# Squares summed on TensorE, VectorE's steps alternated and weight loads in quarters, in the preparation of a two-layer kernel

## The chip, the cores and the metric

The kernel runs on one core of one Trainium2 chip. The metric is the device time of one launch in microseconds (us); a change of less than about 1% can't be told from no change here. All data is 32-bit float in memory; some operands are handed to TensorE in its single-pass form of the same width.

## The reference

The program is a two-layer network on 16 sequences of 512 tokens with 128 features (16 heads of 8). This case touches only what is prepared ahead of layer 0. Cut to what matters:

```python
xn = layernorm(x)                               # per token, 128 features
static = xn @ W.T                               # per token
k = rmsnorm(xn.reshape(B, L, 16, 8)) * k_norm_w # per token and head: root mean square of 8 values
for t in tokens:                                # per sequence and head, an 8 x 8 state S
    S = lam * S
    S = S + beta * outer(k[t], -static[t] - k[t] @ S)
    o[t] = k[t] @ S
x = x + layernorm(static + o) + ffn(xn)         # ffn: five weight matrices, three of them 512 wide
x = x + attention_layer_1(layernorm(x)) + ffn_1(...)
```

## The kernel before, in words

The program has two stages. `prepare` (line 125) makes, for each of the 16 sequences, five arrays of 128 rows by 512 tokens in HBM: the transposed normalized input (xnT), and P, K, R and fac, with which the recurrence over tokens can later be taken in blocks of four. It also turns the five weight matrices of the first feed-forward net into the form that TensorE wants. `recur_and_second_layer` then does the recurrence, both feed-forward nets and the second layer. Only `prepare` is changed.

**A sequence in `prepare`.** It is worked on in four engine-wide steps spread over four rounds. Every engine has one list of instructions, written as a loop over rounds `k`; in round k an engine works on the sequences k, k-1, k-2 and k-3, each at another stage, and semaphores with running counts tie the lists together. An engine never takes an instruction out of turn.

- Sequence k: VectorE takes mean and variance (`statistics` L590, `aggregate` L597), ScalarE the root (`root` L464), VectorE its reciprocal and the offset (L602, L603, L607), ScalarE applies both to the four tiles of 128 tokens (`norm` L470), giving p_xn.
- Still of p_xn: ScalarE squares it (`square` L477, tile p_sq), VectorE sums the squares of each head's 8 values (`square_sums` L613, tile p_ssq of 64 columns), ScalarE takes the root (`root_mean` L481, p_rms), VectorE the reciprocal and the product with p_xn (L618, L623, p_keys).
- TensorE transposes p_xn (`normed` L743, PSUM bank p_ps_x), ScalarE copies it out (L486, p_xnT) and SyncE stores it. TensorE transposes the keys with the places of each block of four sorted (`keys` L751), ScalarE copies them (L494, p_kT). TensorE multiplies xnT by W (`static` L758), ScalarE copies that into p_rr (L499).
- Within a block of four tokens the answer needs products of keys one, two and three places apart (d = 1, 2, 3). VectorE makes them (`products` L634, tile p_prod, three instructions of 384, 256 and 128 columns, one semaphore count behind the last), TensorE sums them over a head with a block matrix of ones (`couplings` L766, bank p_ps_n), ScalarE copies them to p_coup (L509). VectorE solves the triangle for R and GpSimd for P: three sweeps j = 0, 1, 2, each a product (L265) and a sum (L269), 384, 256 and 128 columns wide, and each waits for the one before it. GpSimd also makes P's start (`scaled` L382) and K (`outgoing` L390).
- ScalarE squares the keys (L503), TensorE sums and spreads them (`factors` L776, bank p_ps_f), ScalarE turns them into fac (L516).

**The weights.** Eleven groups of four 128 x 128 squares, one per round from k = 2 on: TensorE transposes a group into the same bank p_ps_f (`weights` L786), ScalarE rounds it (`upper` L521), VectorE makes the rest (`lower` L651). Since fac and the weights share p_ps_f, `weights` of round k waits until ScalarE has read fac of round k out of it (`reuse(pe, fac_ok, ...)`), and all of TensorE's list waits with it. The two 512 x 512 matrices arrive as one load of 1 MB each, issued at k = 1 and k = 4.

**TensorE's round** is: static, couplings, keys, normed, factors, weights. **ScalarE's round** is: std, kT, xnT, rr, rms, fac, xn, w_hi, sq, k2, coup.

**The queue of stores.** SyncE issues nearly all transfers, in the order of its list: in round k the stores of P(k-4), xnT(k-1), fac(k-3), K(k-2), then the load of x(k+2), the store of R(k-3), and weights and small constants. P, K and R each have a small transfer besides (`first_p`, `first_k`, `first_r`: the first 64 columns). A wait in this list holds all that stands behind it. Each array has two buffers, so ScalarE may write p_rr of sequence n only when the store of R(n-2) has landed, and likewise for the others.

`count(each, more)` turns a sequence's number into the count that a semaphore has reached; `at(s, stage)` calls a stage if that sequence exists.

## Time and profile before

| | |
|---|---|
| median of 3 runs | 816.92 us (811.57 to 817.61) |
| the profiled execution | 813.44 us |
| its span, first to last instruction | 811.7 us |
| granted TensorE clock over the span | 0.974 |
| `prepare` | about the first 150 us |
| TensorE / VectorE / ScalarE / GpSimd busy, whole span | 90% / 90% / 73% / 79% |

A timeline gives each instruction's start and duration; neighbours in time that are alike are merged, with their count behind an x. A wait stands in brackets with what ended it. "p_" in front of a tile means that it belongs to `prepare`.
### The profile page before, as it was taken

The numbers are of one execution on the slowest core, as the hardware profiler recorded it, in microseconds if no ns is written. First come the engines' busy times: TensorE is split into PE (matmuls) and PEld (weight loads), VectorE is DVE, ScalarE is ACT, GpSimd is POOL, SyncE is SP. The second block draws the span as 40 slices with busy tenths as digits, with TensorE's granted clock in tenths as the row PEclk, the third lists the DMA queues.
The fourth block names the chain that finished last, engine by engine and source line by source line (L and its number), as shares of the span: only waits on it lengthen the run. The fifth ranks groups of instructions, "written<-read, shape, count | busy, mean of one in ns | idle before, by whom it ended". The sixth has DMA issues, their size and how long they took to land.

```text
span 811.7 us, 13074 instructions
## 1 busy us (share of the span) xinstructions
PE 731.4 (90%) x3325; PEld 515.9 (64%) x3325; DVE 727.2 (90%) x2036; ACT 591.0 (73%) x1363; POOL 644.1 (79%) x640
## 2 busy tenths in 40 slices
PE   4979788699999999999999999986699999999998
PEld 2434344467787888778887788762356666666565
DVE  5979898899999999998998979996578888899887
ACT  7878776789778887887888788785565566666631
POOL 3767788697977897879888779766789778889873
PEclk9999999799999999999999999997999999999999
DMA  6678665600512416161151160510623202211001
GB/s 163 200 240 259 202 207 195 162 14 16 142 39 54 89 39 142 39 143 39 39 103 40 39 143 26 160 32 13 182 69 118 66 27 66 66 53 39 2 27 40
DMA packets 136073, 75.75 MB, mean 93 GB/s; under 512 B 74826, under 2 KB 118860, under 8 KB 136012
## 3 DMA queue, kind: packets, MB, share of 16 engines
q1 hardware_dynamic: 134956, 74.58, 32.9%
q10 hardware_dynamic: 1056, 0.52, 0.2%
q8 instruction: 18, 0.29, 0.1%
q14 instruction: 43, 0.35, 0.1%
HBM read 39.86 MB, written 33.55 MB: 90 GB/s over the span
## 4 chain that ended last, share of the span: by engine, by line
PE 61%; ACT 10%; POOL 4%; issue 3%; DVE 2%; POOLq 0%; DVEq 0%; ACTq 0%
PE f_ps L2266 15%; PE f_ps L2268 10%; PE f_ps L2402 7%; PE f_ps L2303 6%; PE f_ps L2403 6%; PE f_ps L2379 4%; PE f_ps L2273 4%; ACT L1896 2%; ACT f_a L1896 1%; PE r_rec L2431 1%; ACT f_hh L1911 1%; PE r_rec L2437 1%; ACT f_h L1910 1%; DVE l_qs L1321 1%; PE r_rec L2421 1%
## 5 line engine op out<-in xcount | busy, mean ns | idle before, releaser
L1646 POOL TENSOR_TENSOR l_kv<-l_qkv 128x1024 f32<-128x1024 f32 x64 | 124.9, 1956 | 21.6 <-PE f_ps L2403 19.6
L1247 DVE TENSOR_REDUCE r_rec<-r_pg 128x32 f32<-128x288 f32 x256 | 113.0, 441 | 0.6 <-ACT r_pg L1865 0.6
L1518 POOL TENSOR_TENSOR f_hl<-f_h,f_hh 128x512 fp32r<-128x512 f32 x64 | 82.1, 1311 | 33.1 <-ACT f_hh L1911 33.1
L1321 DVE TENSOR_TENSOR l_qs<-f_ps,l_qd 128x1024 f32<-128x1024 f32 x64 | 78.1, 1221 | 27.4 <-PE f_ps L2403 20.8
L1259 DVE TENSOR_REDUCE r_gain<-r_kw 128x64 f32<-128x256 f32 x256 | 102.3, 400 | 0.0
L2266 PE MATMUL f_ps<-f_hh,w_hi 128*128 128x512 f32 x256 | 101.2, 395 | 0.4 <-ACT f_b L1900 0.4
L2266 PE MATMUL f_ps<-f_gh,w_hi 128*128 128x512 f32 x256 | 100.0, 390 | 1.3 <-POOL f_gl L1518 1.2
L1526 POOL TENSOR_TENSOR f_g<-f_a,f_b 128x512 f32<-128x512 f32 x64 | 82.2, 1296 | 22.1 <-ACT f_b L1900 22.1
L1267 DVE SCALAR_TENSOR_TENSOR r_rec<-r_rec,lam,r_gain 128x64 f32<-128x64 f32 x256 | 70.1, 274 | 19.2 <-ACT r_w L1876 19.2
L1518 POOL TENSOR_TENSOR f_gl<-f_g,f_gh 128x512 fp32r<-128x512 f32 x64 | 82.2, 1297 | 4.8 <-ACT f_gh L1906 4.6
L1328 DVE TENSOR_REDUCE l_o_in<-l_qs 128x128 f32<-128x1024 f32 x64 | 77.2, 1211 | 0.6
L2402 PE MATMUL f_ps<-l_kv,tri 128*128 128x512 f32 x128 | 67.8, 611 | 8.3 <-POOL l_kv L1646 5.0
L2268 PE MATMUL f_ps<-f_hl,w_hi 128*128 128x512 f32 x192 | 75.0, 391 | 0.0
L2268 PE MATMUL f_ps<-f_gl,w_hi 128*128 128x512 f32 x192 | 74.7, 389 | 0.0
L2049 ACT ACTIVATE l_qkv<-f_ps 128x384 f32<-128x384 f32 x64 | 31.3, 489 | 56.0 <-PE f_ps L2379 55.3
L1906 ACT ACTIVATE f_gh<-f_g 128x512 fp32r<-128x512 f32 x64 | 41.7, 652 | 38.9 <-POOL f_g L1526 38.1
L2266 PE MATMUL f_ps<-f_xh,w_hi 128*128 128x512 f32 x128 | 53.7, 419 | 14.9 <-ACT f_a L1896 14.9
L2403 PE MATMUL f_ps<-l_kv,tri 128*128 128x512 f32 x128 | 66.9, 605 | 0.0
L1910 ACT ACTIVATE f_h<-f_ps,t 128x512 f32<-128x512 f32 x64 | 44.6, 697 | 22.9 <-PE f_ps L2273 22.6
L2303 PEld LDWEIGHTS f_ps<-w,f_e 128*128 128x128 f32 x512 | 59.7, 192 | 0.8
L2303 PE MATMUL f_ps<-w,f_e 128*128 128x128 f32 x512 | 59.7, 275 | 0.0
L2379 PE MATMUL f_ps<-l_w_second,l_xnT 128*128 128x384 f32 x128 | 54.4, 508 | 3.4 <-ACT l_qkv L2049 2.1
(227 smaller groups left out, 2103.7 us busy)
## 6 DMA issues: line engine op xcount, KB each, us to landing
scratch_xnT<-p_xnT SPq DMA_DIRECT2D x16, 256.0 KB, 2.2
scratch_K<-p_kout SPq DMA_DIRECT2D x16, 256.0 KB, 2.4
scratch_fac<-p_fac SPq DMA_DIRECT2D x16, 256.0 KB, 2.0
scratch_R<-p_rr SPq DMA_DIRECT2D x16, 256.0 KB, 2.9
scratch_P<-p_pp SPq DMA_DIRECT2D x16, 256.0 KB, 2.3
first_x<-scratch_xnT SPq DMA_DIRECT2D x16, 256.0 KB, 3.5
first_xt<-in_L_attn_x_dram SPq DMA_DIRECT2D x16, 256.0 KB, 3.0
scratch_W<-r_w SPq DMA_DIRECT2D x16, 256.0 KB, 4.0
```

The lines of the kernel that those rows point to most:

```text
L1247: dve.tensor_reduce(w_here(g, blk), pg[q][:, at, :, :, :].rearrange("p (v g) i k -> p v g i k", g=G)[:, :, g, :, :], AX.X, ALU.add).then_i ...
L1259: dve.tensor_reduce(of_group(g, gain), of_group(g, kw), AX.X, ALU.add).then_inc(gain_ok, 1)
L1321: dve.tensor_tensor(qs[s % 2][:, :].rearrange("p (h v k) -> p h v k", h=H, k=DH), score_banks(s)[:, :, :].rearrange("p a (h v k) -> p (a h ...
L1518: pool.tensor_tensor(lower, full, upper.bitcast(F32), ALU.subtract).then_inc(done, 1)
L1526: pool.tensor_tensor(g_f[:, j, :], a_f[:, j, :], b_f[:, j, :], ALU.mult).then_inc(gate_ok, 1)
L1646: pool.tensor_tensor(dst, k, v, ALU.mult).then_inc(kv_ok, 1)
L2266: nc.tensor.matmul(bank, c.w_hi[:, weights[k], :], upper[k], start=k == 0, stop=False)
L2268: nc.tensor.matmul(bank, c.w_hi[:, weights[k], :], lower[k], start=False, stop=False)
L2303: ins = nc.tensor.matmul(y_at[:, tokens], e_f[:, k, tokens], c.w3[:, k, :], start=False, stop=t == NT - 1 and k == NB - 1)
L2379: nc.tensor.matmul(ps_q[:, 0:3, :].rearrange("p a b -> p (a b)"), xnT[m % XTS][:, t, :], w_second[:, 0:3 * P], start=True, stop=True).then ...
L2402: nc.tensor.matmul(to[:, 0, :], c.tri[:, :], kv[s % 2][:, 0, :], start=True, stop=True)
L2403: nc.tensor.matmul(to[:, 1, :], c.tri[:, :], kv[s % 2][:, 1, :], start=True, stop=True).then_inc(tri_mm, 1)
```

## The change

1. The squares of a head are summed on TensorE. ScalarE squares the transposed tile straight out of the bank p_ps_x, TensorE multiplies it with 16 columns of the block matrix of ones (four matmuls with 16 moving columns, the squares being the stationary side) back into p_ps_x, and ScalarE takes the root from there. VectorE's sum is gone. In TensorE's round the sums stand between `factors` and `weights`; the next transposes into p_ps_x wait for the root.
2. Half the norm: ScalarE normalizes two tiles of a sequence, VectorE the other two, with a semaphore of its own.
3. VectorE's steps alternate: products, sweeps, scale and norm are interleaved, `statistics` and `aggregate` of sequence k+1 are taken at the end of round k, around the keys.
4. The products and couplings are counted place by place, d = 3 first: TensorE may start on one when it is made, and ScalarE copy it.
5. The weights arrive in quarters of 256 KB (512-byte rows), one per round, each issued when the second before it has landed.
6. SyncE's round is K(k-2), xnT(k-1), P(k-3), fac(k-3), R(k-3), load x(k+2), weights. P(k-3) was stored a round later.

```diff
@@ SyncE @@
                     if s.off >= 2:
                         sp.wait_ge(xn_ok, s.count(1, -1))
+                        sp.wait_ge(xn_half, s.count(1, -1))
...
+                def load_weights(g):
+                    if 2 + 2 <= g < NG - 1:
+                        sp.wait_ge(*arrived(g - 2))
+                    sp.dma_start(*mats[g]).then_inc(arrived(g)[0], 16)
...
                 for k in range(B + 1):
-                    at(of(k - 4), store_p)
+                    at(of(k - 2), store_keys)
                     at(of(k - 1), store_normed)
+                    at(of(k - 3), store_p)
                     at(of(k - 3), store_factors)
-                    at(of(k - 2), store_keys)
+                    at(of(k - 3), store_r)
                     at(of(k + 2), load)
-                    at(of(k - 3), store_r)
                     if k in MATS_AT:
-                        sp.dma_start(*mats[MATS_AT[k]]).then_inc(mat_in[MATS_AT[k]], 16)
+                        load_weights(MATS_AT[k])
@@ ScalarE @@
-                    for t in range(NT):
+                    for t in range(NT // 2):
...
-                def square(l):
-                    act.wait_ge(ssq_ok, l.count(1, 1))
-                    act.wait_ge(xn_ok, l.count(1, 1))
-                    act.activation(sq[:, :, :], xn[l.slot][:, :, :], ACT.Square).then_inc(sq_ok, 1)
+                def square(m):
+                    act.wait_ge(ssq_ok, m.count(1, 1))
+                    act.activation(sq[:, :, :], ps_x[:, :, :], ACT.Square).then_inc(sq_ok, 1)
...
                 def root_mean(m):
                     act.wait_ge(ssq_ok, m.count(1, 2))
-                    act.activation(rms[:, :], ssq[:, :], ACT.Sqrt, bias=c.eps_rms[:, :], scale=1.0 / DH).then_inc(rms_ok, 1)
+                    act.activation(rms[:, :], ps_x[:, 0, 0:NT * H], ACT.Sqrt, bias=c.eps_rms[:, :], scale=1.0 / DH).then_inc(rms_ok, 1)
@@ VectorE @@
+                def norm(l):
+                    dve.wait_ge(nm_ok, l.count(1, 1))
+                    dve.wait_ge(x_tr, l.count(1, 1))
+                    for t in range(NT // 2, NT):
+                        ins = dve.tensor_scalar(xn[l.slot][:, t, :], x_in[l.slot][:, t, :], rstd[:, t:t + 1], nm[:, t:t + 1],
+                                                ALU.mult, ALU.add)
+                    ins.then_inc(xn_half, 1)
...
-                    at(of(k - 1), square_sums)
-                    at(of(k - 3), solve, 0)
+                    at(of(k - 3), solve_product, 0)
                     at(of(k), scale)
+                    at(of(k - 3), solve_sum, 0)
                     at(of(k), offset)
-                    at(of(k - 3), solve, 1)
-                    at(of(k - 2), products)
-                    at(of(k - 3), solve, 2)
+                    at(of(k - 3), solve_product, 1)
+                    at(of(k - 2), products, 0)
+                    at(of(k - 3), solve_sum, 1)
+                    at(of(k), norm)
+                    at(of(k - 2), products, 1)
+                    at(of(k - 3), solve_product, 2)
+                    at(of(k - 2), products, 2)
+                    at(of(k - 3), solve_sum, 2)
                     at(of(k - 1), inverse_rms)
+                    at(of(k + 1), statistics)
                     at(of(k - 1), keys)
+                    at(of(k + 1), aggregate)
@@ TensorE @@
                 def normed(m):
                     pe.wait_ge(xn_ok, m.count(1, 1))
+                    pe.wait_ge(xn_half, m.count(1, 1))
                     pe.wait_ge(xT_ok, m.count(1, 1))
+                    pe.wait_ge(rms_ok, m.count(1, 1))
...
+                def square_sums(m):
+                    pe.wait_ge(sq_ok, m.count(1, 1))
+                    for t in range(NT):
+                        ins = nc.tensor.matmul(ps_x[:, 0, t * H:(t + 1) * H], sq[:, t, :], c.head_ones[:, 0:P:DH], start=True, stop=True)
+                    ins.then_inc(ssq_ok, 1)
...
                 def couplings(n):
-                    pe.wait_ge(prod_ok, n.count(1, 3))
                     pe.wait_ge(coup_ok, n.count(1, 1))
-                    pe.wait_ge(r_step, n.count(SWEEPS, 2 * SWEEPS))
...
+                    for i, d in enumerate(PLACED):
+                        pe.wait_ge(prod_ok, n.count(BLK - 1, 2 * (BLK - 1) + i + 1))
+                        pe.wait_ge(r_step, n.count(SWEEPS, SWEEPS + 2 * i + 1))
...
                     at(of(k - 1), normed)
                     at(of(k - 3), factors)
+                    at(of(k - 1), square_sums)
```

TensorE, one round from the copy of a weight group to the next, before (p_ps_f is the shared bank, p_k the squared keys, p_nath a group of the 512-wide weights):

```order
L786 MATMUL p_ps_f<-ident,p_nath 128x128 x4
L758 MATMUL p_ps_s<-p_xnT,ws_t 128x512
L766 MATMUL p_ps_n<-p_prod,head_ones 128x384
L766 MATMUL p_ps_n<-p_prod,head_ones 128x8x32
L766 MATMUL p_ps_n<-p_prod,head_ones 128x8x16
L751 MATMUL p_ps_k<-by_place,p_keys 128x128 x4
L743 MATMUL p_ps_x<-ident,p_xn 128x128 x4
L776 MATMUL p_ps_f<-p_k,head_ones 128x512
```

and with the change (line numbers are those of the changed file):

```order
L823 MATMUL p_ps_f<-ident,p_nath 128x128 x4
L796 MATMUL p_ps_s<-p_xnT,ws_t 128x512
L804 MATMUL p_ps_n<-p_prod,head_ones 128x8x16
L804 MATMUL p_ps_n<-p_prod,head_ones 128x8x32
L804 MATMUL p_ps_n<-p_prod,head_ones 128x384
L783 MATMUL p_ps_k<-by_place,p_keys 128x128 x4
L775 MATMUL p_ps_x<-ident,p_xn 128x128 x4
L813 MATMUL p_ps_f<-p_k,head_ones 128x512
L789 MATMUL p_ps_x<-head_ones,p_sq 128x16 x4
```

The four sums (p_ps_x<-head_ones,p_sq) stand between factors and weights, and the couplings come smallest first.

ScalarE, from the first root of a round to the rounding of the weights, before:

```order
L464 ACTIVATE p_std<-p_mv,eps_ln 128x4
L494 ACTIVATE p_kT<-p_ps_k,knw 128x512
L486 ACTIVATE p_xnT<-p_ps_x 128x512
L499 ACTIVATE p_rr<-p_ps_s 128x512
L481 ACTIVATE p_rms<-p_ssq,eps_rms 128x64
L516 ACTIVATE p_fac<-p_ps_f,gate 128x512
L470 ACTIVATE p_xn<-p_x,p_nm,p_rstd 128x128 x4
L521 ACTIVATE w_hi<-p_ps_f 128x512
```

and with the change:

```order
L483 ACTIVATE p_std<-p_mv,eps_ln 128x4
L512 ACTIVATE p_kT<-p_ps_k,knw 128x512
L504 ACTIVATE p_xnT<-p_ps_x 128x512
L495 ACTIVATE p_sq<-p_ps_x 128x512
L517 ACTIVATE p_rr<-p_ps_s 128x512
L499 ACTIVATE p_rms<-p_ps_x,eps_rms 128x64
L534 ACTIVATE p_fac<-p_ps_f,gate 128x512
L489 ACTIVATE p_xn<-p_x,p_nm,p_rstd 128x128 x2
```

The squares moved from behind w_hi to behind xnT, and their root now stands behind a sum that TensorE makes after factors; the norm has two instructions and not four, and the rounding of the weights (w_hi) follows it as before.

SyncE's queue, a round in which weights are loaded, before:

```order
L322 DMA first_p<-p_pp 16x8x64
L293 DMA scratch_P<-p_pp 128x512
L293 DMA scratch_xnT<-p_xnT 128x512
L293 DMA scratch_fac<-p_fac 128x512
L311 DMA first_k<-p_kout 16x8x64
L293 DMA scratch_K<-p_kout 128x512
L289 DMA p_x<-in_L_attn_x_dram 128x4x128
L316 DMA first_r<-p_rr 16x8x64
L293 DMA scratch_R<-p_rr 128x512
L344 DMA p_nath<-in_L_ffn_h_w_dram 128x4x512
```

and with the change:

```order
L330 DMA first_k<-p_kout 16x8x64
L307 DMA scratch_K<-p_kout 128x512
L307 DMA scratch_xnT<-p_xnT 128x512
L341 DMA first_p<-p_pp 16x8x64
L307 DMA scratch_P<-p_pp 128x512
L307 DMA scratch_fac<-p_fac 128x512
L335 DMA first_r<-p_rr 16x8x64
L307 DMA scratch_R<-p_rr 128x512
L303 DMA p_x<-in_L_attn_x_dram 128x4x128
L312 DMA p_nath<-in_L_ffn_h_w_dram 128x4x128
```

P of the round stands ahead of fac, R and the load of x; it was the first entry of the next round.

## Rows read from the trace of the kernel before

**Rows 1.** Busy time by stretch: us, engines' busy time (instructions), granted clock, DMA.
```profile
65.00:72.70 7.70, 6.78 (x28) 3.43 (x27) 7.31 (x25) 6.66 (x17) 6.37 (x8) 1.00 0.82 250
119.00:121.00 2.00, 2.00 (x4) 0.84 (x3) 1.86 (x7) 1.91 (x5) 1.92 (x4) 0.50 0.61 222
```

**Rows 2.** Timeline of ScalarE, the copies of the transposed tile; start, duration.
```profile
47.05 0.60 ACT L486 ACTIVATE p_xnT<-p_ps_x 128x512 f32<-128x512 f32 x1
...
58.29 0.60 ACT L486 ACTIVATE p_xnT<-p_ps_x 128x512 f32<-128x512 f32 x1
...
81.35 0.61 ACT L486 ACTIVATE p_xnT<-p_ps_x 128x512 f32<-128x512 f32 x1
...
92.31 0.60 ACT L486 ACTIVATE p_xnT<-p_ps_x 128x512 f32<-128x512 f32 x1
```

**Rows 3.** Timeline of TensorE, one group from 68.26 to 75.95 us.
```profile
68.26 0.63 PE L786 MATMUL p_ps_f<-ident,p_nath 128*128 128x128 f32 x4 [0.92 <-ACT p_fac L516]
68.72 1.96 PE L758 MATMUL p_ps_s<-p_xnT,ws_t 128*128 128x512 f32 x2
70.51 1.48 PE L766 MATMUL p_ps_n<-p_prod,head_ones 128*128 128x384 f32 x6
...
73.15 1.88 PE L776 MATMUL p_ps_f<-p_k,head_ones 128*128 128x512 f32 x2
75.95 0.30 PE L786 MATMUL p_ps_f<-ident,p_nath 128*128 128x128 f32 x1 [0.92 <-ACT p_fac L516]
```

**Rows 4.** Timeline of ScalarE beside it, 72 to 76 us.
```profile
72.08 0.93 ACT L509 ACTIVATE p_coup<-p_ps_n 128x384 f32<-128x384 f32 x3 [0.91 <-PE p_ps_n L766]
...
74.30 0.60 ACT L499 ACTIVATE p_rr<-p_ps_s 128x512 f32<-128x512 f32 x1
74.79 0.34 ACT L481 ACTIVATE p_rms<-p_ssq,eps_rms 128x64 f32<-128x64 f32 x1
75.12 0.69 ACT L516 ACTIVATE p_fac<-p_ps_f,gate 128x512 f32<-128x512 f32 x1
```

**Rows 5.** Group of VectorE's sums, 0 to 180 us: count, busy us, mean ns.
```profile
L613 DVE TENSOR_REDUCE p_ssq<-p_sq 128x64 f32<-128x512 f32 x16 | 10.8, 672 | 1.1 <-ACT p_sq L477 1.1
```

**Rows 6.** The same view of the whole span, a stream of load and matmul pairs.
```profile
L2303 PEld LDWEIGHTS f_ps<-w,f_e 128*128 128x128 f32 x512 | 59.7, 192 | 0.8
L2303 PE MATMUL f_ps<-w,f_e 128*128 128x128 f32 x512 | 59.7, 275 | 0.0
```

**Rows 7.** Timeline of ScalarE: the two long waits for a store.
```profile
50.28 0.60 ACT L499 ACTIVATE p_rr<-p_ps_s 128x512 f32<-128x512 f32 x1 [2.62 <-DMA scratch_R<-p_rr]
...
84.20 0.60 ACT L499 ACTIVATE p_rr<-p_ps_s 128x512 f32<-128x512 f32 x1 [2.25 <-DMA scratch_R<-p_rr]
```

**Rows 8.** Timeline of TensorE: a pause, and the matmuls behind it.
```profile
117.80 2.12 PE L758 MATMUL p_ps_s<-p_xnT,ws_t 128*128 128x512 f32 x2 [2.00 <-issue]
119.74 2.19 PE L766 MATMUL p_ps_n<-p_prod,head_ones 128*128 128x384 f32 x6
```

**Rows 9.** Timeline of GpSimd: first, fourth last and last step of one solution.
```profile
65.41 1.00 POOL L265 TENSOR_TENSOR p_tmp_p<-p_coup,p_pp 128x384 f32<-128x384 f32 x1 [1.17 <-ACT p_coup L509]
...
70.53 1.04 POOL L382 TENSOR_TENSOR p_pp<-p_kT,pfac 128x512 f32<-128x512 f32 x1 [0.51 <-DMA scratch_P<-p_pp]
...
72.06 0.46 POOL L269 TENSOR_TENSOR p_pp<-p_pp,p_tmp_p 128x128 f32<-128x128 f32 x1
```

**Rows 10.** Timeline of SyncE's queue: issue of the stores of R.
```profile
70.28 0.58 SPq L316 DMA_DIRECT2D first_r<-p_rr  x1
70.90 0.59 SPq L293 DMA_DIRECT2D scratch_R<-p_rr  x1
```

**Rows 11.** DMA issues: KB each, median us from issue to landing.
```profile
scratch_R<-p_rr SPq DMA_DIRECT2D x16, 256.0 KB, 2.9
...
p_nath<-in_L_ffn_h_w_dram SPq DMA_DIRECT2D x2, 1024.0 KB, 7.1
```

**Rows 12.** Waits over the span: us in total, times, longest us.
```profile
PE p_ps_f L786 <- ACT p_fac L516: 13.7, 10, 3.4
```

More of the change, by code:

```diff
@@ L139, in prepare @@
     POWERS_AT = 13
+    PLACED = range(BLK - 1, 0, -1)
     with ctx:
@@ L260, in earlier, with sweep_product @@
             return slice(0, (BLK - d) * BSEG)
-        def sweep(eng, n, ap, couplings, tmp, step, j):
+        def sweep_product(eng, n, ap, couplings, tmp, step, j):
             rest = BLK - 1 - j
@@ L506, in couplings @@
                     act.wait_ge(p_step, n.count(SWEEPS, SWEEPS))
[L507 to L508 removed]
+                    for i, d in enumerate(PLACED):
+                        act.wait_ge(n_mm, n.count(BLK - 1, BLK + i))
                         ins = act.activation(coup[n.slot][:, d - 1, :, earlier(d)], in_ps[:, d - 1, :, earlier(d)], ACT.Copy)
```

95 lines of the change are left out of this document (49 added, 46 removed).

## The prediction, blind

> **What bounds the kernel now.** I read the profile's page first: only the first 150 us or so are `prepare`, and the change touches nothing behind them, so the question is how long one round of `prepare` takes and how often it is disturbed. Then I followed one instruction that every sequence has once, ScalarE's copy of the transposed tile: from 58.29 to 81.35 us three rounds pass, so an undisturbed round is 23.06 / 3 = 7.69 us; two rounds took 11.24 (47.05 to 58.29) and 10.96 us (81.35 to 92.31) [rows 2].
>
> Next the busy time of every engine in one round of 7.70 us: VectorE 7.31, TensorE 6.78, ScalarE 6.66, GpSimd 6.37 [rows 1]. By that VectorE looks like the bound, and a reader would expect that taking its sum away (0.67 us a round [rows 5]) pays. But the share isn't the argument; the wait is. TensorE's timeline shows its round without a hole from the transposes of the weights at 68.26 to the end of factors at 73.15 + 1.88 = 75.03, which is 6.77 us, and then one wait of 0.92 us for ScalarE's fac, after which the next round starts at 75.95 [rows 3]. 6.77 + 0.92 = 7.69: this loop is the round. Within the wait, fac starts at 75.12, takes 0.69, and TensorE starts 0.14 behind it [rows 3, 4]. VectorE is nearly as full, but TensorE is never seen waiting for it in this stretch. The same wait stands ten times in the trace, 13.7 us in all [rows 12]: once for each weight group but the first.
>
> The two long rounds each begin with a wait of ScalarE's static copy (p_rr) for an older store of R, 2.62 and 2.25 us [rows 7]. The first lies behind a load of 1 MB, and those took 7.1 us to land against 2.9 for a store of R [rows 11]. They cost 11.24 - 7.69 = 3.55 and 10.96 - 7.69 = 3.27 us, more than the wait, and a later pause shows why: after 2.00 us without work TensorE's couplings took 2.19 us where they took 1.48 undisturbed, at a granted clock of 0.50, which is 1.2 and not 2.4 GHz [rows 1, 3, 8].
>
> **The change part by part.** Everything is put on the profiled execution, 813.4 us (span 811.7 and 1.7 around it), and then on the median of the runs, 816.9, which lies 3.5 above it.
>
> *Squares on TensorE.* Four matmuls are four pairs of 32-bit records with a load each, so 8 loads of 128 x 128 and 8 matmuls of 16 moving columns. The trace has no matmul that narrow with a full load. Nearest is the stream of 512 loads and 512 matmuls of 128 columns: both engines' parts are busy for the same 59.7 us, 0.117 us a pair [rows 6]. Bounds: nothing, if they were free; and if load and matmul followed one another, 8 x (0.192 + 0.275) = 3.7 us [rows 6]. I take the stream's price, since here the loads are the same and the matmuls shorter, and one pair less, since the first load can go in under factors: 7 x 0.117 = 0.82 us. Where it lies decides. The order puts the sums between factors and weights, in TensorE's wait for fac, which would hide them if ScalarE could make fac meanwhile. It can't: in ScalarE's list the root stands ahead of fac, and the root now waits for the sums. So after the sums come the root (fac started 0.33 us behind it, 74.79 to 75.12 [rows 4]) and then fac, and only then the weights. The wait of 0.92 stays whole, and the round becomes 7.69 + 0.82 + 0.33 = 8.84 us. That holds for the ten groups of [rows 12]: 10 x 1.15 = 11.5 us. The first sequence has the same step ahead of its first keys, when nothing else runs: 1.15 us more, bounds 0 and 2.4 (twice it, since TensorE starts at 1.2 GHz and the list of VectorE now has the third tile's statistics ahead of the keys). In the last rounds there are no weights and TensorE has pauses of its own (the 2.00 us of [rows 8]); I take nothing, at most 4 x 0.82 = 3.3.
>
> The Trainium skill speaks against even this price: TensorE: Matmul & The Clock Gate, in the part on packing small matmuls ("What overlaps and what doesn't"), has it that a weight load overlaps a running matmul only when it goes to another row group. By that rule the eight pairs would follow one another, and the sum would be the upper bound above and not 0.82. The stream of [rows 6] uses all rows in each load and still overlaps, so the trace doesn't agree, and I keep the rule as a rival with a small chance.
>
> *VectorE's sum gone, half the norm on it, steps alternated, couplings place by place.* VectorE loses 0.67 [rows 5] and gains two normalizations of 128 columns, at most half of that instruction over 512 columns, 0.34, and at least nothing. ScalarE loses two of four normalizations and copies the couplings as they come. All this shortens ScalarE's and VectorE's lists, and neither is what TensorE's loop waits on except through root and fac, so I count it at nothing. What hides it is the loop above: at 8.84 us a round VectorE's 7.31 leaves 1.5 us. If the loop were not there, up to 0.4 us a round would be to be had.
>
> *Quarters.* The same bytes, in eight loads of 256 KB where there were two of 1 MB. The store of R no longer queues behind 7.1 us of one load, so the first long round should be an ordinary one: -3.4 us. The second has no 1 MB load near it and I leave it in. Bounds: 0 and -6.8.
>
> *P ahead of R in SyncE's queue.* R(k-3) now waits for P(k-3). GpSimd needs from the couplings to P: 65.41 to 72.52, 7.1 us, of which 0.51 was a wait for P's own earlier store [rows 9], so 6.6. Then SyncE issues first_p, P, fac, first_r and R, 0.62 us apart [rows 10], and R lands after 2.9 [rows 11]: 4 x 0.62 + 2.9 = 5.4 at most, about 5.2 as fac's issue is short. ScalarE may then copy p_rr of the sequence two later; from that copy to the end of its couplings were 73.01 + 7.69 - 74.30 = 6.4 us [rows 2, 4], now some 0.5 less as they are copied while they are made. Together 17.7 us for two rounds, 8.85 a round: level with the 8.84 above. So the move costs nothing yet, but has used up the slack: every microsecond that R lands later costs half of one in each round. It gains GpSimd its 0.5 us, which nobody waits for. Value 0, bounds 0 and +11.5 (a landing 2.3 us late in ten rounds, as the waits of [rows 7] show is possible).
>
> Sum: 11.5 + 1.15 - 3.4 = +9.2 us: 822.6 by the profiled execution, 826.1 by the median.
>
> **The rivals.**
>
> *The sums are cheap and both stalls go.* With 16 columns a pair costs half the stream's price, so the round is 7.69 + 0.41 + 0.33 = 8.43, and the longer round gives all stores time: 11 x 0.74 - 6.8 = +1.3, 818. For it: the transfers get 10% more time a round. Against it: the second stall had no large load to blame. Chance 0.20.
>
> *The clock falls in every round.* TensorE's stretch from the end of factors would be 0.82 us of very narrow matmuls and 1.25 us of waiting, 2.1 in all, much like the 2.00 us after which the clock was 0.50 [rows 1, 8]. Couplings would take 0.7 and static 0.16 more [rows 3, 8]: 10 x 0.86 = 8.6, so 834.7. Against it: the narrow matmuls are work of a kind. Chance 0.15.
>
> *R lands late.* The queue's slack is gone, and a landing 2.3 us late costs 1.15 a round: 826.1 + 11.5 = 837.6. For it: the waits of [rows 7]. Against it: rounds are longer and loads smaller. Chance 0.12.
>
> *VectorE was the bound (the other side).* If TensorE's wait for fac only mirrors VectorE, which was busy 7.31 of 7.70, then the sum's 0.67 less the new 0.34 is gained in each of 15 rounds, -5.0, with both stalls -6.8: 805.1. Its place is TensorE's 0.92 us wait, its condition that the sums and the root fit into it, and it decides once a round is below 7.6. Against it is the order of ScalarE's list. Chance 0.08.
>
> *Load and matmul don't overlap.* 3.7 us for the sums, so 11 x (3.7 + 0.33) - 3.4 = +41, 858. Chance 0.03; the page's rule named above would give this.
>
> **How the numbers follow.** The forecast case has 0.42 and its own range, 820 to 832, from the bounds of start and second stall. A change below 1% (8 us, 808.8 to 825.1) can't be told from none. Slower by more: the part of the forecast case above 825.1, 0.25, the clock 0.15, the late store 0.12, the series 0.03: 0.55. Within 1%: 0.17 of the forecast case and the cheap sums' 0.20: 0.37. Faster: 0.08. The range that leaves out no more than 2 in 10 runs from 812 to 840: it leaves out the faster case, the series, and the ends where two costs add up.
>
> **What would show it.** Right: an undisturbed round of about 8.8 us between two copies of the transposed tile; TensorE's wait ahead of the weights still there, 1.2 us, behind about 0.8 us of sums; ScalarE's root waiting for the sums ten times; VectorE idle a microsecond and more a round, waiting for the couplings; no long round at the former 1 MB load. Wrong: a round of 7.7 or less, a root that doesn't wait, a wait for R's store in most rounds (the late store), or a granted clock of 0.50 behind the sums.

## The result, and the profile after

The changed kernel takes 840.24 us (median of 4 runs, 838.93 to 841.48); the kernel before took 814.75 beside it (4 runs). The ratio is 1.032, 95% interval 1.030 to 1.035: slower, where 826.1 with a range of 812 to 840 had been forecast. Its profiled span is 837.2 us.

First the page's row of a round, found as before by ScalarE's copy of the transposed tile (timeline of ScalarE after the change, as [rows 2] before):

```profile
66.41 0.59 ACT L504 ACTIVATE p_xnT<-p_ps_x 128x512 f32<-128x512 f32 x1
...
76.56 0.59 ACT L504 ACTIVATE p_xnT<-p_ps_x 128x512 f32<-128x512 f32 x1
...
86.76 0.59 ACT L504 ACTIVATE p_xnT<-p_ps_x 128x512 f32<-128x512 f32 x1
```

A round takes 10.15 to 10.24 us, not 8.84. The last of the 16 copies starts at 151.85 us; before it was 130.35. So 21.5 of the 25.5 us of span have come by then. The long rounds of [rows 2] are gone: the rounds from the second to the twelfth creep from 9.38 up to 10.24 and none stands out; the last three take 7.55, 9.55 and 7.07.

TensorE's timeline of one round after the change, as [rows 3]:

```profile
69.67 0.63 PE L823 MATMUL p_ps_f<-ident,p_nath 128*128 128x128 f32 x4 [1.07 <-DMA p_nath<-in_L_ffn_h_w_dram]
70.14 1.96 PE L796 MATMUL p_ps_s<-p_xnT,ws_t 128*128 128x512 f32 x2
71.92 2.74 PE L804 MATMUL p_ps_n<-p_prod,head_ones 128*128 128x128 f32 x6
74.45 1.33 PE L783 MATMUL p_ps_k<-by_place,p_keys 128*128 128x128 f32 x8
75.62 0.60 PE L775 MATMUL p_ps_x<-ident,p_xn 128*128 128x128 f32 x4
76.06 1.87 PE L813 MATMUL p_ps_f<-p_k,head_ones 128*128 128x512 f32 x2
77.75 1.01 PE L789 MATMUL p_ps_x<-head_ones,p_sq 128*128 128x16 f32 x8
79.83 0.63 PE L823 MATMUL p_ps_f<-ident,p_nath 128*128 128x128 f32 x4 [1.07 <-ACT p_fac L534]
```

Read by the distance between starts. The sums are where the order put them and take 1.0 us; behind them TensorE waits 1.07 us, for fac as a rule (the first bracket names the quarter of weights, which landed last that time). That part is as forecast. What is not: couplings hold TensorE for 74.45 - 71.92 = 2.53 us, where they took 1.31 undisturbed, and keys for 1.17, where they took 0.89. The windows of the same execution say why (columns: window, length, busy time and count of TensorE, its loads, VectorE, ScalarE, GpSimd, then the granted clock, DMA share, GB/s):

```profile
78.80:79.80 1.00, 0.00 (x0) 0.00 (x0) 1.00 (x4) 1.00 (x3) 0.92 (x3) 1.00 0.16 38
81.00:82.00 1.00, 1.00 (x2) 0.21 (x1) 1.00 (x5) 0.61 (x2) 0.71 (x2) 0.92 0.43 164
82.00:83.00 1.00, 1.00 (x5) 0.83 (x4) 1.00 (x6) 0.22 (x1) 0.00 (x0) 0.50 0.00 0
83.00:84.00 1.00, 1.00 (x4) 0.61 (x3) 0.06 (x1) 0.44 (x2) 0.00 (x0) 0.50 0.64 217
84.00:85.00 1.00, 1.00 (x4) 0.70 (x3) 0.00 (x0) 0.14 (x1) 0.00 (x0) 0.50 0.96 351
```

The clock is still 1.00 in the pause, falls two microseconds behind it, under static, and is 0.50, 1.2 GHz, while couplings run. Couplings hold TensorE for 2.53 us in every round with weights from 50 us on; in the two rounds before that for 1.74 and 2.31 (at 33 and 42 us). With that and with keys, which go from 0.89 to 1.24, the rounds creep up. From 40 to 120 us the clock's mean is 0.83; before it was 0.94:

```profile
40.00:120.00 80.00, 72.12 (x272) 42.98 (x272) 62.34 (x200) 49.38 (x112) 49.87 (x65) 0.83 0.64 204
```

The waits after the change (us in total, times, longest):

```profile
POOL p_tmp_p L267 <- ACT p_coup L527: 46.3, 15, 3.7
...
DVE p_ps_t L267 <- ACT p_coup L527: 26.9, 13, 2.4
...
ACT p_rms L499 <- PE p_ps_x L789: 10.6, 13, 2.0
PE p_ps_f L823 <- ACT p_fac L534: 9.7, 9, 1.1
```

VectorE and GpSimd wait for couplings; the root waits for the sums thirteen times; the wait of [rows 12] is still there, 9.7 us in nine. By this profile the clock looked like the whole miss. A granted clock of 0.50 behind the sums is one of the prediction's own signs of being wrong. The runs show a second cause beside it.

### The profile page after: what moved, and what is told of

Its sections match the earlier page's. It is cut to its first block, busy times and chain, and to the rows that moved or that the text cites. A ratio compares the mean times of both kernels' runs of the same rounds, so it can differ in the third digit from the quotient of the medians.

```text
span 837.2 us, 13366 instructions
## 1 busy us (share of the span) xinstructions
PE 760.8 (91%) x3453; PEld 542.3 (65%) x3453; DVE 733.4 (88%) x2052; ACT 582.8 (70%) x1331; POOL 643.2 (77%) x640
## 4 chain that ended last, share of the span: by engine, by line
PE 59%; ACT 9%; POOL 6%; issue 3%; DVE 1%; POOLq 0%; DVEq 0%
PE f_ps L2304 14%; PE f_ps L2306 9%; PE f_ps L2440 6%; PE f_ps L2341 6%; PE f_ps L2441 6%; PE f_ps L2311 4%; PE f_ps L2417 4%; ACT L1934 2%; POOL l_kv L1684 2%; PE r_rec L2475 1%; PE r_rec L2469 1%; ACT f_hh L1949 1%; ACT f_a L1934 1%; ACT f_h L1948 1%; PE f_ps L2448 1%
## 5 line engine op out<-in xcount | busy, mean ns | idle before, releaser
L267 POOL TENSOR_TENSOR p_tmp_p<-p_coup,p_pp 128x384 f32<-128x384 f32 (+2 forms) x48 | 35.9, 748 | 46.6 <-ACT p_coup L527 46.3
```

## The experiments

Each run has its own runs of the kernel before beside it; ratios are against those, with 95% intervals. "Round" is the distance between two copies of the transposed tile. The diffs are cut to the lines that the argument needs, with some lines joined: declarations, semaphores and the like are left out.

### The clock: e1, e2, e4

**e1_wide**: the sums move 128 columns instead of 16.

```diff
-matmul(ps_x[:, 0, t * H:(t + 1) * H], sq[:, t, :], c.head_ones[:, 0:P:DH], ...)
+matmul(ps_x[:, t, :], sq[:, t, :], c.head_ones[:, :], ...)
...
-act.activation(rms[:, :], ps_x[:, 0, 0:NT * H], ACT.Sqrt, ...)
+act.activation(rms[:, :] ..., ps_x[:, :, 0:P:DH], ACT.Sqrt, ...)
```

The root now reads every 8th column of the sums (DH is 8; the expectation says every 16th).

> The sums of squares move 128 columns instead of 16 (the whole matrix of head ones; the root reads every 16th column). The loads are the same eight, TensorE does more in them. Theory 1 (the sums as such cost about 1 us a round, and the rest of the loss is TensorE's clock, which falls to 0.50 in static and couplings behind sums with hardly any columns and the pause after them): if the wider sums count as work, the granted clock stays 1.00 in couplings, couplings to keys go back from 2.53 to about 1.3 us, and a round takes about 8.9 instead of 10.2: some 822 us. Theory 2 (the pause of 1.1 us behind the sums lets the clock fall, whatever the sums are): round 10.2, 840 us. Theory 3 (the long couplings are a wait for VectorE or ScalarE and not the clock): 840 us, and the clock in them may be either.

Measured 828.5 us, ratio 1.016 (1.012 to 1.019). Most rounds are 8.76. TensorE's timeline in one of them:

```profile
76.09 0.63 PE L823 MATMUL p_ps_f<-ident,p_nath 128*128 128x128 f32 x4 [1.07 <-ACT p_fac L534]
76.56 1.96 PE L796 MATMUL p_ps_s<-p_xnT,ws_t 128*128 128x512 f32 x2
78.34 1.48 PE L804 MATMUL p_ps_n<-p_prod,head_ones 128*128 128x128 f32 x6
79.66 1.05 PE L783 MATMUL p_ps_k<-by_place,p_keys 128*128 128x128 f32 x8
...
82.68 1.09 PE L789 MATMUL p_ps_x<-head_ones,p_sq 128*128 128x128 f32 x8
84.85 0.63 PE L823 MATMUL p_ps_f<-ident,p_nath 128*128 128x128 f32 x4 [1.07 <-ACT p_fac L534]
```

The same eight loads, eight times the columns, the same pause of 1.07 us, and the sums cost 1.1 us instead of 1.0. But couplings are back at 79.66 - 78.34 = 1.32 us, and under them the granted clock is 1.00:

```profile
78.80:79.80 1.00, 1.00 (x6) 0.71 (x5) 0.66 (x3) 0.66 (x2) 0.00 (x0) 1.00 0.15 33
```

So more work for TensorE made the kernel 12 us faster. Theory 2 (the pause alone does it) and theory 3 (a wait) fall. The time is not theory 1's 822 either: behind the second round four took 9.15 to 11.0 us, and ScalarE waited ten times for R's store, 11.8 us in all. In one of these the pause is longer, and there the wide sums don't hold the clock either:

```profile
66.41 0.63 PE L823 MATMUL p_ps_f<-ident,p_nath 128*128 128x128 f32 x4 [1.80 <-DMA p_nath<-in_L_ffn_h_w_dram]
...
68.66 2.40 PE L804 MATMUL p_ps_n<-p_prod,head_ones 128*128 128x128 f32 x6
70.89 1.05 PE L783 MATMUL p_ps_k<-by_place,p_keys 128*128 128x128 f32 x8
```

Behind a pause of 1.80 us couplings hold TensorE for 2.23 us, and the granted clock of the two microseconds from 67 us is 0.54.

**e2_fac_first**: one swap in ScalarE's list.

```diff
-at(of(k - 1), root_mean)
 at(of(k - 3), factors)
+at(of(k - 1), root_mean)
```

> One swap in ScalarE's list: fac (factors of k-3) is copied before the root of k-1, so that TensorE's weights don't wait for a fac that stands behind the root. Theory 1 (the loss is the order root ahead of fac, the pause that it makes and the clock that falls behind that pause): sums run while fac is copied, the pause of 1.07 us is gone, the clock stays 1.00 in couplings, and a round takes 7.8 to 8.0 us: 811 to 816 us, at or below the kernel before. Theory 2 (the sums take TensorE's time and make the clock fall by themselves): the pause is gone but the clock still falls, round 9.2, about 829. Theory 3 (VectorE's half norm, or its list, sets the round): the root is 0.7 us later, keys with it, round 10 or more, 838 and more.

Measured 828.3, ratio 1.018 (1.014 to 1.022): theory 2's number, with theory 1's mechanism. Rounds alternate, 7.68, 9.46, 7.86, 11.14, 7.69, 9.96. In a short one TensorE has no pause and the clock stays 1.00, as theory 1 has it. Each long one begins with p_rr waiting for R's store (eight times, 11.0 us). No theory had named that.

**e4_sums_alone**: the kernel before with only part 1 of the change.

```diff
 # TensorE, round k
 at(of(k - 3), factors)
+at(of(k - 1), square_sums)
 # VectorE, round k
-at(of(k - 1), square_sums)
```

> The kernel before with the first part of the change alone: squares from the transposed tile in PSUM, summed by four matmuls on TensorE between factors and weights, root ahead of fac. Theory 1 (this part alone makes the loss): round of 10.0 to 10.3, granted clock 0.50 in couplings, 838 to 844 us, more where the loads of 1 MB are still in the way. Theory 2 (it takes the other parts as well): 8.8 a round, clock 1.00 in couplings, 825 to 830 us.

Measured 837.8, ratio 1.029 (1.026 to 1.032); rounds creep to 10.24, as in the changed kernel. Theory 1, 0.2 us below its range: this part alone gives nearly the whole loss. The two loads of 1 MB are still in this kernel and no round stands out, so it is the longer round and not the smaller loads that takes the stalls away.

### The queue: e3, e5 to e8, e11

**e3_sums_vector**: the change without its first part (squares from p_xn, summed on VectorE).

```diff
 # TensorE, round k
 at(of(k - 3), factors)
-at(of(k - 1), square_sums)
 # VectorE, round k
+at(of(k - 1), square_sums)
 at(of(k - 3), solve_product, 0)
```

> The change without its first part: the squares come from the normalized tile again and are summed on VectorE; half norm on VectorE, alternated steps, couplings place by place, quarters and SyncE's order stay. Theory 1 (the sums on TensorE with the root ahead of fac are the whole loss): round 7.7, no long round at the load, 812 to 816 us. Theory 2 (the half norm on VectorE costs, 1.78 us where 0.34 was the bound): VectorE has 7.31 + 1.5 us of work a round and sets it, round 8.5 to 8.9, 824 to 832 us.

Measured 828.5, ratio 1.017 (1.015 to 1.020). The number is theory 2's, the mechanism is not: rounds are not 8.5 but 7.63 and 9.99, 7.87 and 10.15, in turn. Its rows in a long one, ScalarE, TensorE, and SyncE's queue ahead of it:

```profile
70.90 0.59 ACT L506 ACTIVATE p_xnT<-p_ps_x 128x512 f32<-128x512 f32 x1
73.28 0.60 ACT L519 ACTIVATE p_rr<-p_ps_s 128x512 f32<-128x512 f32 x1 [1.79 <-DMA scratch_R<-p_rr]
```

```profile
74.84 1.08 PE L825 MATMUL p_ps_f<-ident,p_nath 128*128 128x128 f32 x4 [2.57 <-ACT p_fac L536]
75.71 1.99 PE L798 MATMUL p_ps_s<-p_xnT,ws_t 128*128 128x512 f32 x2
77.52 2.74 PE L806 MATMUL p_ps_n<-p_prod,head_ones 128*128 128x128 f32 x6
```

```profile
66.48 0.41 SPq L307 DMA_DIRECT2D scratch_xnT<-p_xnT  x1
68.52 0.60 SPq L341 DMA_DIRECT2D first_p<-p_pp  x1
69.16 0.58 SPq L307 DMA_DIRECT2D scratch_P<-p_pp  x1
69.79 0.43 SPq L307 DMA_DIRECT2D scratch_fac<-p_fac  x1
70.26 0.55 SPq L335 DMA_DIRECT2D first_r<-p_rr  x1
70.86 0.59 SPq L307 DMA_DIRECT2D scratch_R<-p_rr  x1
```

SyncE stands from 66.9 to 68.5 at first_p, for GpSimd; R is issued at 70.86, 0.04 ahead of the copy of the transposed tile. In the kernel before it was issued at 70.90 [rows 10] with that copy at 73.66, so 2.8 us ahead. R lands late, p_rr waits 1.79, fac is late, TensorE pauses 2.57, and behind that pause the clock falls and couplings take 2.53. This round takes 82.23 - 70.90 = 11.33 us, 3.5 more than the 7.87 ahead of it; the other long rounds with weights, behind waits of 1.2 to 1.9 us, take 10.0 to 10.2, 2.3 more.

**e11_queue_alone**: the kernel before with SyncE's order of the changed one and nothing else.

```diff
-at(of(k - 4), store_p); at(of(k - 1), store_normed); at(of(k - 3), store_factors)
-at(of(k - 2), store_keys); at(of(k + 2), load); at(of(k - 3), store_r)
+at(of(k - 2), store_keys); at(of(k - 1), store_normed); at(of(k - 3), store_p)
+at(of(k - 3), store_factors); at(of(k - 3), store_r); at(of(k + 2), load)
...
 # behind the last round
-store_p(of(B - 3)); store_factors(of(B - 2)); store_keys(of(B - 1)); store_r(of(B - 2)); store_p(of(B - 2))
+store_keys(of(B - 1)); store_p(of(B - 2)); store_factors(of(B - 2)); store_r(of(B - 2))
```

The second half of the diff, the stores behind the last round, belongs to the change too.

> The kernel before with SyncE's order of the changed kernel and nothing else. Theory 1 (R's store, behind P's wait for GpSimd, lands too late wherever rounds want to be 7.7): p_rr waits for it in every second round, TensorE's pause there grows over 2 us, the clock falls to 0.50 behind it, rounds alternate between 7.7 and 10: 826 to 832 us. Theory 2 (the queue has slack without the other parts): 812 to 818 us.

Measured 831.2, ratio 1.020 (1.017 to 1.023): theory 1. Rounds 7.68 and 10.5 to 11.7 in turn, seven waits for R's store of 18.5 us in all. An order of issues, with no work added or taken away, costs 17 us.

**e5_fac_first_old_queue** and **e6_vector_old_queue**: e2 and e3 with SyncE's order of the kernel before, that is with the diff of e11 read backwards.

> fac ahead of the root on ScalarE, and SyncE's order of the kernel before (P a round later, behind nothing; R behind the load). With fac first alone every second round was long (7.7 and 9.5 to 11.1 us), and each long one began with ScalarE's p_rr waiting for the store of R. Theory 1 (the store of R behind P's wait for GpSimd causes these): the waits for R's store all but go, rounds are 7.7 to 7.9 us, clock 1.00 in couplings, 806 to 812 us, below the kernel before. Theory 2 (the long rounds come from the half norm on VectorE or the alternated steps, which make R late itself): they stay, 826 to 830 us.

> Sums back on VectorE, and SyncE's order of the kernel before. Theory 1 (the store of R behind P's wait is what made every second round 10 us there): rounds of 7.7 to 7.9, 806 to 814 us. Theory 2 (VectorE is full with the half norm, which took 1.78 us: 7.31 + 1.5): rounds of 8.5 and more, 822 to 830 us.

e5: 813.9, ratio 1.001 (1.000 to 1.002), level with the kernel before rather than below it. Rounds are 7.70 and 7.87 with one of 10.03, and p_rr waits for R once, 0.8 us. e6: 817.8, ratio 1.005 (1.003 to 1.006); nine rounds are 7.6 to 8.0 and five stay long, 9.2 to 10.5, here and there and no longer in turn. The queue made the alternation in both: theory 1, with its numbers 2 to 4 us too low.

TensorE's weights in a short round of e3, where VectorE makes the sums, have the old wait of 0.92 us in front of them:

```profile
65.32 0.63 PE L825 MATMUL p_ps_f<-ident,p_nath 128*128 128x128 f32 x4 [0.92 <-ACT p_fac L536]
```

In a short round of e5 the sums fill it:

```profile
43.79 1.01 PE L790 MATMUL p_ps_x<-head_ones,p_sq 128*128 128x16 f32 x8
44.89 0.63 PE L824 MATMUL p_ps_f<-ident,p_nath 128*128 128x128 f32 x4
```

No bracket stands behind the weights: TensorE no longer waits. So the sums fit into the wait, as my rival on the other side had it, once fac does not stand behind the root. They gain nothing there, since they are as long as the wait was. The clock holds in these rounds, with the same 16 columns in the sums: couplings take 48.45 - 47.13 = 1.32 us in the round of these rows.

**e7_old_queue**: the changed kernel with only SyncE's order put back (the same lines as in e5).

> The changed kernel with SyncE's order of the kernel before and nothing else. Theory 1 (in the changed kernel R's store isn't late, since its rounds of 10.2 give it time; the pause behind the sums and the clock make the rounds): rounds of 10.2 as before, 838 to 841 us. Theory 2 (the late store of R is in every round): 828 us or less.

Measured 832.0, ratio 1.024 (1.022 to 1.025), between the two. The rounds up to the thirteenth are the same, 10.2 us, so a round of 10.2 does give R's store time and theory 1 holds for them. What it missed is the end: the fourteenth round takes 8.17 instead of 9.55, and from the last copy of the transposed tile to the last store of P go 168.23 - 150.18 = 18.1 us instead of 172.99 - 151.85 = 21.1. In the changed kernel SyncE stands first for K (issued at 164.05) and then for P (167.48) before it comes to the last stores, and p_rr waits for R's store, 1.23 and 2.13 us, where it waits 0.20 and 0.51 in e7. Behind such a wait TensorE pauses and the clock falls here too (the changed kernel, ScalarE and TensorE):

```profile
155.06 0.60 ACT L517 ACTIVATE p_rr<-p_ps_s 128x512 f32<-128x512 f32 x1 [2.13 <-DMA scratch_R<-p_rr]
155.75 2.02 PE L796 MATMUL p_ps_s<-p_xnT,ws_t 128*128 128x512 f32 x2 [1.71 <-issue]
157.59 2.74 PE L804 MATMUL p_ps_n<-p_prod,head_ones 128*128 128x128 f32 x6
```

The last store of P is issued 172.99 - 168.23 = 4.8 us earlier in e7, of 7.7 us of span; the other 2.9 lie behind `prepare`. From that store to the end of the span go 664.2 us in the changed kernel and 661.3 in e7. The kernel before has 663.1 and the other profiled executions lie between 661 and 664.5, so the 2.9 are not shown to come from the queue.

**e8_fac_first_r_first**: fac first, and of SyncE's new order only P moved behind R.

```diff
-at(of(k - 3), store_p)
 at(of(k - 3), store_factors)
 at(of(k - 3), store_r)
+at(of(k - 3), store_p)
```

> fac ahead of the root on ScalarE, and in SyncE's new order only P moved: behind fac and R instead of ahead of them. Theory 1 (P ahead of R is the harmful part of the new order): as with the whole old order, rounds of 7.7 to 7.9, 806 to 812 us. Theory 2 (K's stores, now first in the round, hold the queue for GpSimd just as well: SyncE waited 22.9 us for K and 19.7 us for P): between the two, 815 to 828 us.

Measured 815.2, ratio 1.002 (1.000 to 1.004). The number stands at the lower end of theory 2's range; but it is 1.3 us above e5 and 13.1 below e2, and the rounds are theory 1's, 7.68 to 7.98 from the third to the thirteenth with one of 10.06. So moving P behind R takes nearly all of the queue's cost away. K's stores at the head of the round hold SyncE for 35.2 us in thirteen waits, and p_rr still waits for R only twice, 1.9 us in all. What K's place costs by itself is not shown, since e8 also has R ahead of the load and e5 has not.

### Both causes taken away: e16

**e16_wide_old_queue**: the edit of e1 and SyncE's old order together.

> The changed kernel with the wide sums (128 columns) and SyncE's order of the kernel before: with the clock held and R's store early, this is the case that I had forecast. Theory 1: rounds of 8.77 throughout, none of 10 to 11, and the 6 to 8 us that the old order gave the end: 816 to 822 us. Theory 2 (the clock falls in some rounds for another reason than the wait for R's store): 824 to 828.

Measured 821.05, ratio 1.009 (1.007 to 1.012), span 819.3. Ten rounds of 8.76, none longer behind the second; the clock never leaves 1.00 between 40 and 120 us:

```profile
40.00:120.00 80.00, 71.40 (x311) 40.09 (x309) 71.77 (x231) 56.89 (x129) 57.79 (x75) 1.00 0.71 229
```

This is the case that I had forecast: 8.76 for 8.84 a round, and 6.6 us above the kernel before for +9.2.

### The other parts: e9, e10, e15

**e9_quarters_alone**: the kernel before, 1 MB loads cut into quarters.

```diff
-MATS_AT = {1: 2, 4: 3, 7: 4}
+MATS_AT = {g - 1: g for g in range(2, NG)}
...
-(nath[:, 0, :, :], io["L0_ffn_h1_w"].rearrange("(o p) i -> p o i", p=P)),
+mats += [(nath[:, w, :, i * P:(i + 1) * P], rows[:, :, i * P:(i + 1) * P]) for i in range(NB)]
```

> The kernel before with its two loads of 1 MB cut into eight of 256 KB, one a round, and nothing else. Theory 1 (my term of the prediction: the first long round has the 1 MB load ahead of R's store, the second has not): one long round instead of two, -3.4 us, 811 us by the runs here. Theory 2 (both long rounds come from R's store being at the edge whatever is loaded): no gain, 812 to 816 us.

Measured 814.7, ratio 0.9993 (0.9975 to 1.0012): theory 2. The long rounds 11.24 and 10.96 become 9.11 and 10.55, but the second round goes from 7.26 to 8.27.

**e10_half_norm_alone**: the kernel before, two of four tiles normalized on VectorE.

```diff
 # VectorE, round k
 at(of(k - 2), products)
+at(of(k), norm)
 at(of(k - 3), solve, 2)
 # ScalarE's norm
-for t in range(NT):
+for t in range(NT // 2):
```

> The kernel before with two of the four tiles normalized on VectorE (behind the products), and nothing else. Theory 1 (those two steps take 0.8 us each beside GpSimd's, so VectorE's 7.31 of 7.69 becomes 8.9 and it sets the round): rounds of 8.4 to 8.9, 820 to 830 us. Theory 2 (they take long only where VectorE is in no hurry): 0.34 each, rounds of 7.7 to 8.0, 813 to 818 us.

Measured 823.0, ratio 1.010 (1.007 to 1.012): theory 1, at the low end. Its group of VectorE's half norm (count, busy us, mean ns):

```profile
L623 DVE TENSOR_SCALAR p_xn<-p_x,p_rstd,p_nm 128x128 f32<-128x128 f32 x24 | 13.4, 596 | 0.0
```

1.19 us a round for the two; rounds are mostly 8.0 to 9.8, and from 20 to 125 us VectorE is busy for 99.2 of the 105. Where VectorE is full, this part costs 8.6 us. In the changed kernel VectorE idles 2 us a round, so the part should be hidden there; no run takes it out of the changed kernel. e6, which has the half norm with the alternated steps, the couplings place by place and the quarters, is 4.3 us above the kernel before, so these three together give back some 4 of the 8.6.

**e15_sums_alone_fac_first**: e4 with fac ahead of the root, by the swap of e2.

> The kernel before with the sums on TensorE and fac ahead of the root, so with neither the alternated steps nor the couplings place by place. It tells what these two do. Theory 1 (nothing, TensorE's own work of 7.7 us sets the round): as fac first with the old queue, rounds of 7.7 to 7.9 and now and then a long one by the loads of 1 MB, 814 to 819 us. Theory 2 (the later root needs the alternated steps, or the couplings wait for all products together and TensorE gets a new pause there): rounds of 8.3 and more, 822 us and more.

Measured 818.5, ratio 1.006 (1.004 to 1.009): theory 1. Undisturbed rounds are 7.70 here and 7.70 and 7.87 in e5, so the alternated steps and the couplings place by place gain nothing in the steady round. But e5 also has the half norm and the quarters, which e15 has not, so what each does by itself isn't shown. Over the whole kernel e5 is 4.6 us faster, by its first round (8.29 for 9.12) and because fewer rounds are long. Against e4, 837.8, the one swap is worth 19 us.

### Attempts to beat both: e12, e13, e14

**e12_normed_behind_factors**: kernel before, quarters, and TensorE's transposes of the normalized tile moved into its wait.

```diff
-at(of(k - 1), normed)
 at(of(k - 3), factors)
+at(of(k - 1), normed)
```

> An attempt to beat both: the kernel before with the quarters, and with the transposes of the normalized tile moved on TensorE from ahead of factors to behind them (fac ahead of the copy of the transposed tile on ScalarE), so that they lie in TensorE's wait of 0.92 us for fac. Theory 1 (the round is TensorE's 6.77 us of work and that wait): TensorE's round becomes 6.77 + 0.48 = 7.25, VectorE with 7.31 sets it, rounds of 7.3 to 7.45, 3 to 4 us less: 807 to 810. Theory 2 (the copy of the transposed tile, now behind fac, comes late for static and makes the wait there): rounds of 7.7 or more, 812 and more.

Measured 817.0, ratio 1.003 (1.002 to 1.005): theory 2's number and its place, static, but another copy than it names. The wait for fac halves, and static gets one of its own. Static also waits until p_rr has emptied its bank, and with fac and the transposed tile ahead of it that copy (65.09 + 0.60) ends 0.10 us before static starts, 0.5 behind that of the transposed tile:

```profile
64.86 0.63 PE L800 MATMUL p_ps_f<-ident,p_nath 128*128 128x128 f32 x4 [0.48 <-ACT p_fac L530]
65.79 2.02 PE L772 MATMUL p_ps_s<-p_xnT,ws_t 128*128 128x512 f32 x2 [0.30 <-issue]
```

```profile
64.61 0.60 ACT L500 ACTIVATE p_xnT<-p_ps_x 128x512 f32<-128x512 f32 x1
65.09 0.60 ACT L513 ACTIVATE p_rr<-p_ps_s 128x512 f32<-128x512 f32 x1
```

The steady round is 7.77; one of 10.36 has a wait for R's store.

**e13_stores_spread**: kernel before, quarters, R's store ahead of the load, and three copies that stood together in one round spread over three.

```diff
-at(of(k + 2), load)
 at(of(k - 3), store_r)
+at(of(k + 2), load)
...
-if k == 8: first_x, first_xt, gamma
+if k == 6: first_x
+if k == 9: gamma
+if k == 11: first_xt
```

> An attempt to beat both: the kernel before with the quarters, R's store put ahead of the load in SyncE's round, and the three copies for the second layer, which stood together in one round (the ninth), spread over three rounds. Theory 1 (the two long rounds left in the kernel with quarters alone, 9.11 and 10.55 us, come from R's store landing behind other transfers): both go, all rounds are 7.7, 806 to 809 us. Theory 2 (they come from elsewhere or only move): 811 to 815.

Measured 809.5, ratio 0.994 (0.992 to 0.996): 5.0 us less than the kernel before and 30.8 less than the changed one. The first is under the 1% named at the start, though the interval leaves out no change. Rounds three to twelve are 7.63 to 7.69 but for one of 8.03. Theory 1, for the three edits together: the quarters alone gave 0.1% (e9), and the order and the spreading were not taken apart.

**e14_fac_first_spread**: e5 with e13's edits of the queue.

> The changed kernel with fac ahead of the root, SyncE's order of the kernel before, R's store ahead of the load and the three copies spread. Theory 1: the one round of 10.03 us that fac first with the old queue still had goes, 810 us or a little more, 3 us above the last one by its slow first two rounds (8.29 and 9.38 against 7.39 and 8.27) and its 7.78 a round. Theory 2 (the long round only moves): 812 to 815.

Measured 810.3, ratio 0.996 (0.994 to 0.998): theory 1. From the third round on to the thirteenth no round is longer than 7.87.

## Why the prediction was wrong, and where it was right

The miss is 840.2 - 826.1 = 14.1 us. It is made of three sizes, each the difference of two runs and known to some 2 us: e7 to e16 (the clock) +10.9; the changed kernel to e7 (the queue) +8.2; and the forecast case itself, which came out at 821.05, -5.0, of which 2.5 is that the kernel before ran at 814.5 here and not at the 816.9 on which I had put it. Taken in the other order, from the changed kernel to e1 (11.8) and from e1 to e16 (7.4), the two causes have about the same sizes. Two of my rivals came true at once, the clock and the late store, and the range left out by its own words the ends where two costs add up.

- **The sums and the root, 1.15 us a round: right.** The round with the clock held is 8.76 for 8.84. Its two terms are each off by 0.2 and cancel: the sums take 1.0 and not 0.82, and TensorE then waits 1.07 and not 1.25. The order of ScalarE's list decides it, as argued: with fac first (e5, e15) the same sums add next to nothing to a steady round.
- **"The clock falls in every round", left as a rival at 0.15 and priced 8.6 us: the step that failed.** The 8.84 us of the forecast hold only at full clock, and that was assumed because the narrow matmuls "are work of a kind". e1 shows that behind a pause of 1.07 us they did not hold the clock and matmuls of 128 columns did. The size was short too: I took 0.16 from static and 0.7 from couplings [rows 8]. Measured is nothing in static, 2.53 - 1.31 = 1.22 in couplings and some 0.3 in keys, 1.4 a round in all (10.2 to 8.76, with wide sums 0.1 longer). The forecast's own row of a pause of 2.00 us with its fallen clock [rows 8] was the nearest row there was, and by the rule that I used elsewhere, to go by the nearest row, this should have been the forecast.
- **P ahead of R, value 0: the second step that failed; the working was right, the value wrong.** Two rounds of 17.7 us were worked out. e3 has 7.87 + 9.99 = 17.86 and 7.87 + 10.15 = 18.0, e1 at 8.76 a round waits for R ten times, and e11 has 18.2 to 19.4. But I compared this with a round of 8.84 and no more: I did not ask what happens in the last rounds, where no round of 8.84 protects it (e7: 4.8 us), nor wrote down that the queue would cost 17 us in a kernel whose other parts worked. In the changed kernel, with its rounds of 10.2 us, about half of that shows, 8.2 us. My rival's price of 11.5 us came near by luck: it had R late in ten rounds, and p_rr waited for R three times.
- **First rounds, +1.15: short by 2.** The first two rounds of e16 are 8.48 and 9.40 where they were 7.39 and 7.26, +3.2 (bound given: 2.4). Why is open: e3, with no sums on TensorE, has 8.02 and 10.00, and e4, with the sums and nothing else, 9.11 and 9.44.
- **The stalls, -3.4 with bounds 0 and -6.8: wrong part credited.** Quarters alone gain 0.6 +- 1.5 us (e9). In the changed kernel both long rounds did go, but the longer rounds did that (e4 keeps the loads of 1 MB and has no long round either), as one of my rivals said; at 7.7 a round it took e13's edits of the queue besides.
- **The forecast case came near partly by luck.** Up to the last copy of the transposed tile e16 is 8.1 us behind the kernel before: the ten steady rounds +10.7, the first two +3.2, both stalls gone -6.8, the last three rounds +0.9. The forecast had +11.5, +1.15, -3.4 and 0.
- **Half the norm, at most 0.34 a round: wrong by five.** It is 1.78 us in the changed kernel. That it cost nothing there is argued from VectorE's idle time and not shown by a run.
- **VectorE was the bound, 0.08: rightly low.** e15 takes VectorE's sum away and hides it in TensorE's wait, and its undisturbed round is 7.70, not shorter.
- **Load and matmul one after the other, 0.03: rightly low.** Eight loads with their matmuls take 1.0 us, where one after the other they would take 3.7. The rule of the Trainium skill that the prediction names (TensorE: Matmul & The Clock Gate, "What overlaps and what doesn't"), that a weight load overlaps a running matmul only in another row group, is not borne out by this row either.

## What to carry to other kernels

A narrow matmul is cheap in its own time and can still be dear: look at what TensorE does around a place that already has a pause, and price the clock's fall over the stages behind it, not in the pause alone. When work moves to another engine, put what the next engine waits for ahead of what the moved work delays; here one swap of two lines was worth 19 us. In a queue of transfers the one store whose landing is waited for goes ahead of stores that wait for a slow engine: the opposite cost 17 us (e11). The gains over the kernel before, 5 and 4 us, came with that store ahead of a load and with smaller and spread transfers (e13, e14).

## What the runs showed of the hardware

**VectorE's time beside GpSimd.** The half norm in the first sequence, while GpSimd does nothing, and in a later round (timeline of VectorE after the change), with GpSimd beside the later one:

```profile
8.67 0.60 DVE L632 TENSOR_SCALAR p_xn<-p_x,p_rstd,p_nm 128x128 f32<-128x128 f32 x2
...
57.30 1.78 DVE L632 TENSOR_SCALAR p_xn<-p_x,p_rstd,p_nm 128x128 f32<-128x128 f32 x2
```

```profile
57.28 1.03 POOL L408 TENSOR_TENSOR p_kout<-p_kT,kfac 128x512 f32<-128x512 f32 x1
58.28 0.72 POOL L267 TENSOR_TENSOR p_tmp_p<-p_coup,p_pp 128x256 f32<-128x256 f32 x1
```

0.30 us each alone, 0.89 each beside GpSimd. Taken singly, the first of the pair ends at 58.40 and the second at 59.08, each about 0.1 us behind the end of one of GpSimd's instructions (58.31 and 59.00). The Trainium skill, in SBUF — State Buffer, "Who interferes with whom", has VectorE, in the two-port modes that a tensor_scalar can enter, share a pair of ports with GpSimd, and whichever issues first keeps it for its whole instruction. The rows agree with that. By them the bound for two tiles should have been two GpSimd instructions, about 1.8 us a round, and not 0.34.

**The clock behind narrow matmuls.** What stands ahead of couplings, and how long they then hold TensorE (to the start of keys); 1.3 us is full clock, 2.5 half:

| sums | pause before the next matmuls | couplings | where |
|---|---|---|---|
| none | 0.92 us | 1.31 us | kernel before, 70.51 |
| 16 columns | none | 1.32 us | e5, 47.13 |
| 16 columns | 0.81 us | 2.54 us | changed kernel, 140.07 |
| 16 columns | 1.07 us | 2.53 us | changed kernel, 71.92 |
| 128 columns | 1.07 us | 1.32 us | e1, 78.34 |
| 128 columns | 1.80 us | 2.23 us | e1, 68.66 |
| none | 2.57 us | 2.53 us | e3, 77.52 |

So neither a short pause nor the narrow sums did it by themselves; together they did: 0.81 us behind narrow sums was enough, and 0.92 us without them was not. In e3, with the longest pause, the clock fell within the pause (0.76 from 73.40 to 74.40 us, then 0.50), and in the changed kernel only two microseconds behind it. A pause of just 1.07 us without any sums was not tried.
